# Convolution groups 1 to 13: the first level of the product sum as an accumulating DMA, the second on GpSimd

## What is computed

```python
# x, ctx: (8, 256, 512); viewed as (8, 32, 8, 512) = b, h, i, l; k: (32, 512)
kv  = xn[:, :, :, None, :] * ctx[:, :, None, :, :]      # xn = layernorm(x); 8 x 8 pairs (i, j) for each h
y   = causal_conv(kv, k) + kv * skip                    # along the 512 positions, one filter for each h
att = einsum('bhijl,bhil->bhjl', y, ctx)                # sum over the 8 i
x   = x + tanh(g_xattn) * att
h   = layernorm(x)
expert = argmax(h @ router_w)                           # one of 8 for each row
x   = x + tanh(g_ffn) * (silu(h @ gate[expert]) * (h @ up[expert])) @ down[expert]
```

## Time and profile before

| | us |
|---|---|
| median of 3 runs (lowest, highest) | 677.65 (677.15, 678.43) |
| the profiled execution | 677.27 |
| its span, first to last instruction | 675.50 |
| TensorE busy in the span | 640.0 (95%) |
| GpSimd busy | 554.6 (82%) |
| VectorE busy | 513.8 (76%) |
| ACT busy | 236.5 (35%) |

### The profile page before, as it was taken

The page is one execution under the profiler, slowest core; times in us unless marked ns, Lnnn a source line. Parts: engine busy times, 40 slices in busy tenths (PEclk is TensorE's granted clock), DMA queues, the critical chain, the costliest instruction groups (busy, mean ns, idle before and its releaser), DMA issues.

```text
span 675.5 us, 10934 instructions
## 1 busy us (share of the span) xinstructions
PE 640.0 (95%) x3203; PEld 532.3 (79%) x3204; DVE 513.8 (76%) x659; ACT 236.5 (35%) x346; POOL 554.6 (82%) x354
## 2 busy tenths in 40 slices
PE   7999999999999999989697999999999999999984
PEld 6787888888888888778576878888888888888873
DVE  6878888888888888677799958699999939541510
ACT  5444444433334443252231332233333333322320
POOL 3999999999999999848375978888898878785842
PEclk9999999999999999998798999999999999999998
DMA  7454555555555655557477646367766645441110
GB/s 221 136 185 142 186 190 181 183 183 188 188 188 188 188 172 173 189 207 264 145 230 261 208 156 223 118 209 227 230 216 209 224 151 174 143 146 38 46 51 18
DMA packets 51906, 117.77 MB, mean 174 GB/s; under 512 B 5900, under 2 KB 6092, under 8 KB 51888
## 3 DMA queue, kind: packets, MB, share of 16 engines
q1 hardware_dynamic: 43728, 99.68, 45.7%
q0 software_dynamic: 4320, 12.72, 5.3%
q10 hardware_dynamic: 3840, 5.15, 2.8%
HBM read 94.08 MB, written 25.02 MB: 176 GB/s over the span
## 4 chain that ended last, share of the span: by engine, by line
PE 66%; DVE 14%; POOL 8%; issue 8%; DMA 2%; ACT 1%; DVEq 0%; ACTq 0%; SPq 0%; POOLq 0%
PE pair L1467 24%; PE bank L1356 20%; PE bank L1483 13%; POOL sorted_x L497 3%; PE pair L1390 3%; POOL kv_lo L748 2%; DVE prod L1183 2%; DVE kv L1115 2%; PE bank L1498 2%; PE pair L1326 2%; DVE up L1270 1%; POOL prod L772 1%; DVE down_hi L1270 1%; PE bank L1440 1%; DVE up L1273 1%
## 5 line engine op out<-in xcount | busy, mean ns | idle before, releaser
L1356 PE MATMUL bank<-kv_hi,strip 128*128 128x512 f32 x640 | 210.8, 398 | 1.1 <-DVE kv_lo L1138 0.9
L1356 PEld LDWEIGHTS bank<-kv_hi,strip 128*128 128x128 f32 x640 | 120.2, 188 | 26.5 <-DVE kv_lo L1138 1.1
L748 POOL TENSOR_TENSOR kv_lo<-kv,kv_hi 128x2048 fp32r<-128x2048 f32 x30 | 138.6, 4621 | 2.1 <-issue 1.2
L1356 PE MATMUL bank<-kv_lo,strip 128*128 128x512 f32 x320 | 124.6, 389 | 0.0
L1151 DVE TENSOR_TENSOR prod<-bank,cT 128x512 f32<-128x512 f32 x128 | 85.0, 683 | 22.3 <-PE bank L1356 22.3
L926 ACT ACTIVATE kv_hi<-kv 128x2048 fp32r<-128x2048 f32 x30 | 57.6, 1919 | 110.3 <-DVE kv L1115 85.8
L1467 PE MATMUL pair<-up,xT_hi 128*128 (+1 forms) x288 | 89.8, 393 | 5.1 <-DVE up L1273 5.1
L1467 PE MATMUL pair<-gate,xT_hi 128*128 (+1 forms) x288 | 91.0, 397 | 2.1 <-issue 1.8
L1356 PEld LDWEIGHTS bank<-kv_lo,strip 128*128 128x128 f32 x320 | 60.3, 188 | 11.2
L1115 DVE TENSOR_TENSOR kv<-pair,cK 128x2048 f32<-128x2048 f32 x30 | 68.4, 2280 | 0.0
L1467 PEld LDWEIGHTS pair<-up,xT_hi 128*128 128x128 f32 x288 | 54.7, 190 | 16.9 <-issue 5.5
(11 more groups left out here) (193 smaller groups left out, 1159.3 us busy)
## 6 DMA issues: line engine op xcount, KB each, us to landing
raw<-gate_w SPq DMA_DIRECT2D x32, 512.0 KB
raw<-down_w SPq DMA_DIRECT2D x32, 512.0 KB
strip<-kparts SPq DMA_DIRECT2D x15, 1024.0 KB, 6.0
raw<-up_w SPq DMA_DIRECT2D x28, 512.0 KB
sorted_x<-fill SPq DMA_DIRECT2D x14, 792.0 KB, 4.7
xs<-sorted_x ACTq DMA_DIRECT2D x19, 256.5 KB
x_in<-x_back SPq DMA_DIRECT2D x16, 256.0 KB, 4.7
cK<-ctx_back SPq DMA_DIRECT2D x16, 256.0 KB, 4.8
```

Source lines behind the costliest of these rows:

```text
L748: nc.gpsimd.tensor_tensor(kv_lo[u][:, hh, :], kv[:, hh, :], kv_hi[u][:, hh, :].bitcast(f32), ALU.subtract).then_inc(s_klo, 1)
L1356: last = nc.tensor.matmul(y_bank[lb][:, :], strip[u][:, 2 * hh + t, d * P:(d + 1) * P], v[u][:, hh, mb * COL:(mb + 1) * COL], start=(mb == ...
```

## The change

- Groups 1 to 13: `sum_pairs` takes the place of `add_pairs`. When all products of the group are there, GpSimd writes a one-element marker and issues a DMA within SBUF that adds terms 4 to 7 to terms 0 to 3 (1 MB to 1 MB). `sum_fours`, the second level, is now GpSimd's too; it waits for that DMA and stands between the two halves of the next group's preparation. Group 14 keeps GpSimd's pair sum and VectorE's add of fours.
- `kv_low` no longer waits for the add of fours.
- VectorE: the outer product of head 0 comes before product 1 and the skip sum. The residual and second norm come after product 2 of head 1.
- TensorE: `x2_in(g-2)` comes after blocks 0 to 2 of head 0, where the logits were; logits of g-2 and head sums of g-1 come before the last block of head 1. The last stage has an order of its own.
- ACT: the copy of the transposes after `kv_high` of head 0, the logits' copy after the first norm.

```diff
+                def sum_pairs(g, u):
+                    eng.wait_ge(s_p, (g + 1) * 2 * LB)
+                    nc.gpsimd.tensor_tensor(mark_pool[:, 3:4], ones[:, 0:1], ones[:, 0:1], ALU.mult)
+                    nc.gpsimd.dma_start(prod[u][:, 0:J // 2, :], prod[u][:, J // 2:J, :], accum_op=ALU.add)\
+                        .then_inc(s_pairs, 16)
+
+                def sum_fours(g, u):
+                    eng.wait_ge(s_pairs, 16 * g)
+                    nc.gpsimd.tensor_tensor(prod[u][:, 0:2, :], prod[u][:, 0:2, :], prod[u][:, 2:4, :], ALU.add)\
+                        .then_inc(s_add2, 1)
...
                 def kv_low(g, u, hh):
                     h = 2 * g + hh
                     eng.wait_ge(s_khi, h + 1)
-                    if hh == 0:
-                        wait(eng, s_add2, g - 2)
...
                             add_half_pairs(0, 0, 0)
+                        elif hh == 0 and known(g, lambda g: g >= 3):
+                            sum_fours(g - 2, u)
...
+                    elif isinstance(g, int) and g == G - 1:
+                        add_pairs(g - 1, 1 - u)
                     elif known(g, lambda g: g >= 2):
-                        add_pairs(g - 1, 1 - u)
+                        sum_pairs(g - 1, 1 - u)
...
                     product(g, u, n, 0, 0)
                     if first:
                         outer(1, 1, 0, 0)
+                    elif more:
+                        outer(g + 1, 1 - u, n + u, 0)
                     product(g, u, n, 0, 1)
                     skip_sum(g, u)
-                    if more and not first:
-                        outer(g + 1, 1 - u, n + u, 0)
                     product(g, u, n, 0, 2)
-                    if known(g, lambda g: g >= 2):
+                    if final:
                         add_fours(g - 1, 1 - u)
...
+                    else:
+                        product(g, u, n, 1, 0)
+                        product(g, u, n, 1, 1)
+                        if not (first or second):
+                            product(g, u, n, 1, 2)
+                        if before:
+                            residual(g - 1, 1 - u, n - 1 + u)
+                            ln2_first(g - 1, 1 - u)
+                            ln2_last(g - 1)
+                        if second or first:
+                            product(g, u, n, 1, 2)
                     product(g, u, n, 1, 3)
...
+                    if isinstance(g, int) and g == G - 1:
+                        conv(g, u, n, 0, (0, 1))
+                        x2_in(g - 2, u)
+                        conv(g, u, n, 0, (2,))
+                        logits_of(g - 2)
+                        skip_turn(g, u)
+                        conv(g, u, n, 0, (3,))
+                        sum_heads(g - 1, 1 - u)
...
+                        return
+                    conv(g, u, n, 0, (0, 1, 2))
+                    if first:
+                        v_in(1)
+                    elif not second:
+                        x2_in(g - 2, u)
                     if not first:
                         skip_turn(g, u)
                     conv(g, u, n, 0, (3,))
                     if first:
                         skip_turn(g, u)
-                    if before and not second:
-                        sum_heads(g - 1, 1 - u)
...
+                    conv(g, u, n, 1, (0, 1))
                     if second:
                         sum_heads(0, 0)
-                    conv(g, u, n, 1, (2, 3))
+                    if first or second:
+                        conv(g, u, n, 1, (2, 3))
+                    else:
+                        conv(g, u, n, 1, (2,))
+                        logits_of(g - 2)
+                        sum_heads(g - 1, 1 - u)
+                        conv(g, u, n, 1, (3,))
                     if known(g, lambda g: g < G - 2):
                         v_in(g + 2)
-                    if before:
-                        x2_in(g - 1, 1 - u)
```

More of the change, by code:

```diff
@@ L958, in stage @@
                     if known(g, lambda g: g >= 2):
+                        xn2T_out(g - 2)
+                    if not more:
                         logits_out(g - 2)
@@ L965, in stage @@
                         norm1(g + 2, u)
+                    if more and known(g, lambda g: g >= 2):
+                        logits_out(g - 2)
                     if isinstance(g, int) and g == G - 1:
@@ L1180, in add_fours @@
                 def add_fours(g, u):
-                    dve.wait_ge(s_add, G + 2 if isinstance(g, int) and g == G - 1 else g + 2)
+                    dve.wait_ge(s_add, 3)
                     nc.vector.tensor_tensor(prod[u][:, 0:2, :], prod[u][:, 0:2, :], prod[u][:, 2:4, :], ALU.add)\
@@ L1215, in stage @@
                     second = isinstance(g, int) and g == 1
-                    if second:
+                    if final:
+                        residual(g - 1, 1 - u, n - 1 + u)
                         product(g, u, n, 1, 0)
-                        product(g, u, n, 1, 1)
-                    if before:
[L1220 to L1223, removed]
                         places_first(dve)
-                    if before:
                         ln2_first(g - 1, 1 - u)
                         ln2_last(g - 1)
-                    if not second:
                         product(g, u, n, 1, 1)
-                    if final:
                         dve.wait_ge(s_count_up, 1)
@@ L1233, in stage @@
                         choose(dve, range(3))
-                    product(g, u, n, 1, 2)
-                    if final:
+                        product(g, u, n, 1, 2)
                         choose(dve, range(3, 7))
+                    else:
[4 more added lines that the diff above has]
+                        if before:
+                            residual(g - 1, 1 - u, n - 1 + u)
+                            ln2_first(g - 1, 1 - u)
+                            ln2_last(g - 1)
+                        if second or first:
+                            product(g, u, n, 1, 2)
                     product(g, u, n, 1, 3)
@@ L1364, in logits_of @@
                     wait(pe, s_logc, g)
-                    pe.wait_ge(s_skc, min(g + 2, G) if isinstance(g, int) else g + 2)
+                    if isinstance(g, int) and g >= G - 3:
+                        pe.wait_ge(s_skc, min(g + 2, G))
+                    else:
+                        pe.wait_ge(s_skc, g + 3)
                     for b in range(LB):
@@ L1374, in skip_turn @@
                     wait(pe, s_skc, g)
+                    wait(pe, s_logc, g - 2)
                     nc.tensor.matmul(skip_bank, flip[:, :], skip_r[:, u, :, :].rearrange("p a h -> p (a h)"),
@@ L1400, in stage @@
                 def stage(g, u, n):
[L1401 to L1406, removed]
                     first = isinstance(g, int) and g == 0
                     second = isinstance(g, int) and g == 1
+                    if isinstance(g, int) and g == G - 1:
[6 more added lines that the diff above has]
+                        sum_heads(g - 1, 1 - u)
+                        conv(g, u, n, 1, (0,))
+                        count_first(pe)
+                        conv(g, u, n, 1, (1, 2, 3))
+                        x2_in(g - 1, 1 - u)
+                        return
[4 more added lines that the diff above has]
+                        x2_in(g - 2, u)
                     if not first:
```

11 lines of the change are left out of this document (5 added, 6 removed).

## The result

| | before | after |
|---|---|---|
| median (lowest, highest), us | 677.40 (675.76, 678.43) | 708.74 (704.39, 712.41) |
| profiled execution, its span | 677.27, 675.50 | 708.32, 706.6 |
| TensorE, GpSimd, VectorE busy | 640.0, 554.6, 513.8 | 654.2, 527.7, 494.4 |

The change makes the kernel **slower by 4.6%**, ratio 1.046 (95% interval 1.044 to 1.048), four runs of each. The forecast was 679.8 with a range to 692, so the result lies outside it; of the rivals the first, the late transfer, came nearest.

A forecast was written before the change was run, and what follows sets the result against it. GpSimd was taken to set the pace, TensorE close behind. Terms -3.9 + 6.5 + 0.6 - 1.0 = +2.2 us on 677.27 gave 679.5, on the median 679.8; own range 678.6 to 682, 80% range 674.5 to 692.

The forecast's parts named there:

- the late transfer: First rival: transfer lands at 12.0 us, twice the strip row, 2.5 over its cover; about 712 us; chance 0.25.
- The wait on the tree, 3.9 us: Stages 2 to 14: TensorE's head sums waiting on the adds cost 3.9 us, which relieving GpSimd would remove.
- GpSimd's new stage, 15.8: GpSimd's work per stage falls from 17.4 to 15.8 us, so it stops being the bound.
- The transfer, 9 us, covered up to 9.5: GpSimd's DMA within SBUF lands 9 us after issue, between bounds 6.0 and 12.0; up to 9.5 costs nothing.
- One for one: Landing beyond the 9.5 us cover delays GpSimd, second split, next issue and TensorE's head sums by the same amount.
- The stop at the turn, 6.5: TensorE waits 0.5 us for VectorE's later skip sum in each of 13 stages, 6.5 us in all.
- Ends and passes: Stage 1 +0.6 us, stage 15 -1.0; TensorE's loss at four loop passes, about 0.28 each, counted in the stages.
- The rule beside it: Skill's rule that a reducing transfer runs at about half a copy's rate; by it the first rival would be the forecast.

The follow-up runs named there:

- e9: Changed kernel with half the pair sum by a 0.5 MB adding transfer, half on GpSimd, skip sum early, VectorE adding fours behind the first norm: 680.22 us, ratio 1.004.
- e13: e9 with one add of fours, that of group 1 in stage 2, moved from VectorE to GpSimd: 676.40 us, ratio 0.995 to the kernel before.
- e2: Changed kernel with a plain copy in place of the adding transfer, so the sum leaves out terms 0 to 3: 695.94 us, ratio 1.027.
- e6: Changed kernel with the next group's 1 MB strip load held until the adding transfer has landed: 688.11 us, ratio 1.018.
- e5: Changed kernel with half the bytes: the transfer adds only terms 4 and 5 to 0 and 1; terms 6 and 7 left out: 696.63 us, one execution.
- e3: Changed kernel's order without a transfer: GpSimd adds the pairs, VectorE the fours: median 684.19 us, ratio 1.008.
- e10: Control of e9 without a transfer, the whole pair sum on GpSimd: median 702.29 us of seven runs from 691.5 to 713.5, no ratio.
- e1: Changed kernel with VectorE's skip sum moved ahead of the outer product, transfer left as it was: 714.64 us, ratio 1.054.
- e4: Changed kernel with ten dummy transposes on TensorE filling the wait before the head sums: 698.68 us, ratio 1.030.

## Why the prediction was wrong, step by step

- **The wait on the tree, 3.9 us.** Right, and shown late: e9 and e13 have stages of 17.0 (forecast 17.07 without the wait) with TensorE busy in 140.00 of 140 us.
- **GpSimd's new stage, 15.8.** Right enough: 199.32 / 13 = 15.3. Issue 0.88 for my 1.0, fours 2.35 for 2.37.
- **The transfer, 9 us, covered up to 9.5.** This step failed. The cover was about right: 9.8 in the stage above; in e2 8.6 cost nothing, in e6 10.1 cost 6.3 us of waiting in nine stages. The size was not: 11.2, near the bound of 12.0 that I had set and passed over for the middle. I had taken the strip's 6.0 as a sum of everything. It has two parts that the row couldn't show, and the table above has them: 2.5 for adding and 3.5 for the traffic of the same microseconds. I had even named the traffic, as something the strip's row contained already. But a transfer that is itself part of what is in flight meets the strip, and the store, which went from 6.0 to 9.0 to land, says so from the other side.
- **"One for one" beyond the cover.** Right: 13 x (11.2 - 9.5) = 22 by the forecast's cover, 18 measured, which is GpSimd's wait for the transfer, 18.4 in 13 stages. The chain I named, second split and next issue, is the one that closes the ring at full clock.
- **The clock.** Not in the prediction at all, 10 us. I had priced a stop at its own length; in seven stages one of 1.2 us was followed by a fall that made the stage 1.5 longer. 0.5 at the turn alone (e2, e5) was followed by no fall.
- **The stop at the turn, 6.5.** Right: 9.9 us of waiting in 15 stages on TensorE's loads, 17.57 or 17.58 a stage in e2, e3 and e5.
- **Ends and passes.** Stage 1 +1.0 for +0.6, last stage -0.9 for -1.0. The 1.1 for the loop's passes did not show in e2.
- **The rule beside it.** The first rival had it that adding doubles the transfer, and its time of 712 was near the result. The traces agree with the direction, not with twice the landing: with SP's loads held, adding took 7.7 for the copy's 5.2, 1.5 times. The Trainium skill, "Collectives: The Full Stack", section "The bandwidth ceiling: the fold count and why AG ≠ RS ≠ AR", has half the rate for a transfer that reads two sources. End to end this is 1.5 here. Whether the part of the 5.2 that moves data was doubled, no run here shows. The larger part of the lateness was traffic. The rival's 712 was luck: it had 6.0 for adding where 2.5 was measured, nothing for the traffic where 3.5 was, and 32 us of lateness where there were 18, with 10 of clock beside them.

What stays open: what the 6.2 us that don't go with the bytes are made of besides the traffic, which of SP's transfers makes how much of the 3.5, why the clock fell behind some stops of 1.2 us and not behind others, and what lets some of VectorE's adds in between two GpSimd additions and shuts others out. None of these was tried by itself.

## What to carry to other kernels

A transfer put in place of an engine's work has to be priced with what flies beside it: find the loads that will be in the air in its microseconds and take the far bound, not the middle, where the nearest row is a plain load. Where the engine that issues the transfer also waits for it, close the ring from issue to issue, over each of its branches, before adding up stops, and price each stop of TensorE that recurs every stage with a possible fall of the clock. Moving half the bytes gave stages of 17.0 and fitted into the cover; the whole did not.

## What the runs showed of the hardware

- Landing of a 1 MB transfer within SBUF, issued by GpSimd: 5.2 us as a copy and 7.7 adding, beside a 256 KB load only; 8.6 and 11.2 beside a 1 MB load and smaller transfers; 0.5 MB adding 8.7 to 8.9 beside the same. Its issue took 0.88 us on GpSimd adding, 0.59 as a copy.
- A VectorE addition with both inputs in SBUF that started 0.9 before the end of GpSimd's `kv_low` ended 1.1 after that end (2.00 long); where it was not let in before GpSimd's next instruction it took 7.5 to 9.8 (one in e3, one in e9, five in e10). The Trainium skill, "SBUF — State Buffer", section "SBUF: two separate sides", says that the port pair shared by the two engines is an exclusive lock, held for the whole instruction. The rows agree on the lock, and add that the loser can wait for several instructions of the other: 8.83 us over two `kv_low` and a `skip_first`.
- TensorE's granted clock fell to half for 3.4 us after idle waits of 1.2 us at the head sums in seven of 13 stages, and in twelve of 13 in e1, where most were 1.8 or 1.9; not once in the stages of e4, where transposes that nobody reads filled the same wait.
